# VectorE's order inside one step of a graph attention network: input statistics and mask sum at the head, score minima ahead of the norm, second statistics behind low half 6

## The reference, cut to what matters

```python
h = jnp.maximum(_layernorm(x, axis=-1), 0.0)
x = x + _L0_gnn_ref(h, adj, W_fc, W_attn)      # one attention layer
h = jnp.maximum(_layernorm(x, axis=-1), 0.0)
x = x + _L1_gnn_ref(h, adj, ...)               # three attention layers

# _L0_gnn_ref
h = graph_input @ W_fc.T;  f1 = h @ a1;  f2 = h @ a2
scores = leaky_relu(f1[:, :, None] + f2[:, None, :], 0.2)
attn = softmax(where(adj == 0, -1e9, scores), axis=2)
return elu(attn @ graph_input)

# _L1_gnn_ref, for each of the three layers l
si = x @ attn_w[l, :d];  sj = x @ attn_w[l, d:]
scores = leaky(si[:, :, None] + sj[:, None, :] + attn_b[l], 0.2)
attn = softmax(where(adj + eye > 0, scores, -inf), axis=-1)
h = layernorm(x + attn @ x, g1[l], beta1[l])
ff = gelu(h @ W1[l] + b1[l]) @ W2[l] + b2[l]   # 256 -> 1024 -> 256
x = layernorm(h + ff, g2[l], beta2[l])
```

## Time and profile before

| | |
|---|---|
| median of 3 runs | 2773.87 us (2773.44 to 2774.45) |
| the profiled execution | 2771.33 us, its span 2769.5 us |
| TensorE busy (matmul) | 2651.5 us, 96% of the span |
| ScalarE busy | 2200.2 us, 79% |
| VectorE busy | 2138.1 us, 77% |
| GpSimd busy | 1689.8 us, 61% |
| TensorE's mean granted clock | 0.985 of full speed |

### The profile page before, as it was taken

The page is one execution under the profiler, slowest core; times in us unless marked ns, Lnnn a source line. Parts: engine busy times, 40 slices in busy tenths (PEclk is TensorE's granted clock), DMA queues, the critical chain, the costliest instruction groups (busy, mean ns, idle before and its releaser), DMA issues.

```text
span 2769.5 us, 53308 instructions
## 1 busy us (share of the span) xinstructions
PE 2651.5 (96%) x16771; PEld 2386.7 (86%) x16868; DVE 2138.1 (77%) x7995; ACT 2200.2 (79%) x4494; POOL 1689.8 (61%) x2197
## 2 busy tenths in 40 slices
PE   3699999999999999999999999999999999999997
PEld 2488888988888989888888888889888998998997
DVE  5898878777878777878777878777878777676674
ACT  4699888888888888888887888888878777777774
POOL 4467666566766565566676666555677554454655
PEclk8699999999999999999999999999999999999999
DMA  5221322222222221122222122222222211111111
GB/s 177 90 70 62 95 81 92 66 79 76 87 81 77 66 71 62 64 70 88 85 90 69 65 67 76 69 68 68 80 89 91 62 45 52 35 52 52 51 64 54
DMA packets 118589, 203.43 MB, mean 73 GB/s; under 512 B 12800, under 2 KB 85536, under 8 KB 118304
## 3 DMA queue, kind: packets, MB, share of 16 engines
q1 hardware_dynamic: 118304, 199.97, 22.3%
HBM read 116.05 MB, written 83.89 MB: 72 GB/s over the span
## 4 chain that ended last, share of the span: by engine, by line
PE 71%; DVE 12%; POOL 8%; issue 5%; ACT 3%; DMA 0%; DVEq 0%; SPq 0%; POOLq 0%; ACTq 0%
PE bank L605 32%; PE bank L588 26%; PE ps_u L564 7%; POOL xo L374 3%; DVE g_lo L983 3%; DVE st L957 2%; PE ps_u L646 2%; POOL rs L1283 2%; DVE ub L1074 2%; PE ps_s L559 2%; PE ps_s L551 1%; POOL hb L374 1%; DVE vb L952 1%; DVE ub L952 1%; ACT g_hi L859 1%
## 5 line engine op out<-in xcount | busy, mean ns | idle before, releaser
L605 PE MATMUL bank<-w_hi,g_hi 128*128 128x256 f32 x3072 | 890.5, 290 | 15.3 <-DVE g_lo L983 15.1
L605 PE MATMUL bank<-w_hi,g_lo 128*128 128x256 f32 x3072 | 865.2, 282 | 0.0
L605 PE MATMUL bank<-w_lo,g_hi 128*128 128x256 f32 x3072 | 863.9, 281 | 0.0
L859 ACT ACTIVATE g_hi<-bank,b_eff 128x512 fp32r<-128x512 f32 x768 | 529.3, 689 | 334.4 <-PE bank L588 327.9
L983 DVE TENSOR_TENSOR g_lo<-bank,g_hi 128x512 fp32r<-128x512 f32 x768 | 518.9, 686 | 202.3 <-ACT bank L861 188.2
L588 PE MATMUL bank<-zt_hi,w_hi 128*128 128x512 f32 x1536 | 632.4, 412 | 12.0 <-DVE g_lo L983 5.6
L588 PE MATMUL bank<-zt_hi,w_lo 128*128 128x512 f32 x1536 | 607.7, 396 | 0.0
L588 PE MATMUL bank<-zt_lo,w_hi 128*128 128x512 f32 x1536 | 606.4, 395 | 0.0
L605 PEld LDWEIGHTS bank<-w_hi,g_hi 128*128 128x128 f32 x3072 | 578.9, 188 | 24.2 <-DVE g_lo L983 23.1
L605 PEld LDWEIGHTS bank<-w_lo,g_hi 128*128 128x128 f32 x3072 | 579.2, 189 | 0.8
L605 PEld LDWEIGHTS bank<-w_hi,g_lo 128*128 128x128 f32 x3072 | 578.7, 188 | 0.0
(11 more groups left out here) (95 smaller groups left out, 4145.8 us busy)
## 6 DMA issues: line engine op xcount, KB each, us to landing
xb<-x_scratch SPq DMA_DIRECT2D x88, 512.0 KB, 4.0
x_scratch<-xo SPq DMA_DIRECT2D x64, 512.0 KB, 4.8
xin<-in_x SPq DMA_DIRECT2D x38, 512.0 KB, 5.9
r_scratch<-elu_r SPq DMA_DIRECT2D x32, 512.0 KB, 3.0
xin<-r_scratch SPq DMA_DIRECT2D x32, 512.0 KB, 4.6
out<-xo SPq DMA_DIRECT2D x32, 512.0 KB, 3.4
m<-m_scratch SPq DMA_DIRECT2D x96, 128.0 KB, 3.8
x_scratch<-h SPq DMA_DIRECT2D x24, 512.0 KB, 2.9
```

What stands on the lines that cost most here:

```text
L605: mm = pe.matmul(y, g[:, c, r * P:(r + 1) * P], w[:, l, c, :], start=(c == 0 and n == 0), stop=(c == C - 1 and n == 2))
L859: act.activation(g_hi[:, c, :], block_in, ACT.Gelu, bias=bias).then_inc(g_hi_ready, 1)
```

## The change

VectorE's list is changed in all steps that don't take the first branch, so from step 5 on. `input_statistics()` (early steps) and `mask_sums()` (middle steps) move to the head of the step, ahead of `g_low(0)`. `input_variance()` moves up behind `first_variance()`, `input_shift()` behind `first_norm()`. `g_low(2)` now stands ahead of the score minima `next_lows()`, `g_low(3)` ahead of `first_norm()`. `second_statistics()` stands behind `g_low(6)`, which comes one place further forward, and `second_variance()` behind `g_low(7)`. GpSimd's list has the root of the input norm ahead of `scaled_rows()`. The lists of TensorE, ScalarE and SyncE are the same as before.

```diff
+                input_statistics()
+                if v1 is not None and early_step(v1) >= 0:
+                    mask_sums(v1)
                 g_low(0)
                 sum_rows()
                 g_low(1)
                 first_variance()
+                input_variance()
+                g_low(2)
                 next_lows()
-                g_low(2)
+                g_low(3)
                 first_norm()
-                g_low(3)
-                input_statistics()
+                input_shift()
                 g_low(4)
                 g_low(5)
+                g_low(6)
                 second_statistics()
-                g_low(6)
+                g_low(7)
                 second_variance()
-                g_low(7)
-                input_variance()
-                if v1 is not None and early_step(v1) >= 0:
-                    mask_sums(v1)
                 low_rows()
-                input_shift()
...
                 first_root()
                 if v3 is not None and v3 < CH:
                     made_root()
-                scaled_rows()
-                if v3 is not None and v3 < CH:
+                    scaled_rows()
                     input_root()
                     second_root()
                 else:
+                    input_root()
+                    scaled_rows()
                     second_root()
-                    input_root()
```

## The result

The changed kernel takes 2864.38 us (median of four runs, 2860.79 to 2870.03) against 2773.65 us (four runs, 2771.57 to 2774.45). The ratio is 1.033 (95% interval 1.0312 to 1.0348). The profiled execution took 2860.79 us with a span of 2859.0, that is 89.5 us more than the span before.

A forecast was written before the change was run, and what follows sets the result against it. TensorE, busy for 96% of the span, was taken to bound the kernel. 2771.33 (profiled execution) + 50 (early steps) + 19 (middle steps) = 2840, expected as a median of 2843; range for 8 in 10: 2813 to 2878.

The forecast's parts named there:

- the stall: Early steps: statistics wait for x, g_low(1) is late, TensorE stalls 2.7 us at hidden(4); +50 us over 23 steps.
- the middle steps: Middle steps: VectorE's lateness carries over and the mask sum loses its cover; 26.90 becomes 28.0, together +19 us.
- 2830 to 2862: The forecast case's own range for the whole kernel's time, chance 0.68.
- the clock rival: Early-step stalls each bring a stretch at half clock costing 1.65 us, 38 in all; time 2881, chance 0.12.
- three signs: Wrong if x statistics start within 1 us of vb, middle steps stay at 26.9, or the clock dips in early steps.
- The landing of x: Early steps: x lands 4.8 us into step 35, with 0.2 added on the mean for later loads.
- The landing that the Trainium skill: Early steps: x lands 3.2 us after its issue, stall 1.2 us shorter, sum some 27 us smaller.
- The rest at nothing: Late steps, steps without side work, GpSimd's moved root and SyncE's later xb load cost nothing.
- The rival on the other side: g_low(0) of early steps: x is there in time, leaving a gain of 27 us; 2746 in all, chance 0.04.
- The mask sum: Head of middle steps: the time behind g_low(7) that hid it is gone; 0.70 us plus 0.61 to the next start.

The follow-up runs named there:

- filler kernel: The changed kernel with eleven matmuls of 128x512 more ahead of hidden(4) in early steps, into a bank nobody reads then: 2843.28 us, ratio 1.0254.
- kernel without the wait: The changed kernel with the head statistics of early steps taken over old h0 rows already there, in place of x: 2764.15 us, ratio 0.9965.
- statistics put back: The changed kernel with statistics, variance and shift of x and GpSimd's input root back in their old places: 2783.34 us, ratio 1.0035.
- low halves kept: As statistics put back, with the mask sum and second statistics also behind g_low(7), so only the moved low halves 2 and 3 stay: 2779.92 us, ratio 1.0019.
- low halves alone: The kernel before with only g_low(2) moved ahead of the score minima and g_low(3) ahead of the norm: 2775.18 us, ratio 1.0004.

## Why the prediction was right, and where it was off

The forecast was 2843 with a range of 2813 to 2878, and slower with 0.94. Measured were 2864. Its cause is shown: with the moved statistics alone 86 us come, and with the wait alone taken away they go. Its sizes were off by 21 us, in three terms: +6 for the stall, +32 for the clock, -19 for the middle steps. The last 2 us lie outside the 69 steps.

That the total is no further off is in part luck, since two of these errors have opposite signs. The measured time lies above the forecast's own 2830 to 2862, and inside the wide range because that was drawn up towards the clock rival. Of the three signs that I had named for being wrong, two came: middle steps stay at 26.9, and the granted clock dips in the early steps. The late x was forecast rightly, what TensorE does behind its stall was not.

**The landing of x and the stall: right.** Forecast were 4.8 us into step 35, and 0.2 later on the mean. In step 35 VectorE's wait ended at 4.55. On the mean of all 23 it ended at 5.25 (the sum `vb` ends 0.91 into a step, and the row of waits gives 99.8 / 23 = 4.34 of waiting). At full clock a step is as long as this landing plus a constant: step 68 waited until 2102.96, 4.75 into the step, and took 29.06, so the constant is 24.31 (the other six steps at full clock give 24.30 to 24.31). With it 23 steps at full clock make 23 x (5.25 + 24.31) = 680 us. The filler kernel, which kept the clock, has 679.7. Against 624.3 before that is **+56**, where the sum had +50. The late landings, which the earlier trace rows told of, put the mean 0.7 behind step 35 and not 0.2; that step 35 itself came 0.25 sooner took a part of it back. The page after has nearly the same median:

```profile
xin<-in_x SPq DMA_DIRECT2D x38, 512.0 KB, 6.0
```

The landing that the Trainium skill (DMA: Bandwidth & Descriptors, Anatomy of one DMA) gave, by an estimate from its figures (1.2 us sooner, and 27 us off the sum), was not seen: no early step waited for less than 4.5 us into it.

**The clock: the step that failed.** The forecast said "granted clock still 1.00 from 135 us on" and gave 0.12 to the rival in which it falls. It fell in 16 of 23 early steps and costs 712.1 - 680 = **+32 us** there. Added up step by step it is 30; the rest is time that step 47, the last of the hardware loop's first turn, loses in the filler kernel too. The rival's own term was 38, from 1.65 a step in all 23. Ten falls cost about that, six cost 2.3 to 2.7 (step 32 is one, 32.70 long), and seven steps had none. The bound was the weak point: 2.45 us without work in step 47 had been harmless, and I took 2.8 for near it. But 2.45 is the sum of what step 47 had. The longest single wait of TensorE in the 69 steps of the kernel before is shorter (the view of the earlier trace rows):

```profile
PE bank L588 <- issue: 1.9, 1, 1.9
```

The waits for low half 1, 2.3 to 4.1 us each by the rows, were all longer, and not harmless in most cases. The kernel before had shown nothing about a single wait of this length. The Trainium skill (TensorE: Matmul & The Clock Gate, Why this matters for your kernels) says that idle gaps bring the engine back to the lower clock; 16 steps agree with it, seven with waits as long do not.

**The middle steps: mis-sized, +19 forecast and 0 measured.** The delay of the chain was right. GpSimd's `hb` (answers to the earlier trace rows) was forecast for 1117.6, 15.5 into step 35, and starts 15.0 into it:

```profile
1159.01 2.84 POOL L374 TENSOR_TENSOR hb<-ub,g_row 128x256 f32<-128x256 f32 x4 [2.02 <-DVE ub L1074]
```

`nm` of the second norm stood 19.12 into step 35 before, and stands 22.29 into it now, 3.17 later (3.2 forecast), with 9.88 to `vb` behind it (9.99 forecast):

```profile
1166.30 0.16 DVE L973 SCALAR_TENSOR_TENSOR nm<-mv,rs 128x4 f32<-128x4 f32 x1
...
1176.18 1.29 DVE L1180 TENSOR_TENSOR vb<-bank,hb 128x512 f32<-128x512 f32 x2
```

But TensorE was late as well, and by more: step 35 grew by 3.4 us, so `vb` starts 1.77 into step 36 and not at the forecast 3.25, and that step takes the 26.90 of before. Where the clock held, the lateness did arrive, at less than half the size forecast: step 15 takes 27.35 and not 28.0.

```profile
541.25:570.66 29.41, 26.48 (x171) 23.69 (x170) 22.77 (x88) 21.86 (x44) 17.33 (x22) 1.00 0.28 86
570.66:598.01 27.35, 27.10 (x176) 24.23 (x175) 23.84 (x96) 23.56 (x51) 18.57 (x24) 1.00 0.21 73
```

There the step before had grown by 2.6, nearly as much as VectorE was late. With the clock kept everywhere (the filler) the middle steps cost +11. The layer-2 middle steps gained 2.6 us together (step 18 takes 27.51), which pays for steps 6, 9 and 12, of 0.4 us more each, for step 15, and for step 48, of 1.1 more. So two of my terms were tied: what the clock adds in an early step it takes from the middle step. Together they are +32 and -11. The forecast's 2843 is what the filler kernel measured (2843.28): where the clock holds, stall and middle steps make 66 us (1974.17 - 1907.94), against the 69 of the sum.

**The rest at nothing: right.** Late steps take 28.44, the steps from 74 on 26.3.

**The rival on the other side: its price was wrong.** If x had been there in time I gave 2746, a gain of 27 us made of all the waits for low halves. The kernel without the wait has 2764, the one with only the low halves moved 2780. The early and the middle step are bound as a pair by VectorE's and GpSimd's chain from the norm to `vb`. What TensorE no longer waits for in the early step, it waits for at `vb` in the middle step, unless that chain is made shorter too. This error of mine showed in four expectations: statistics put back (2754 expected, 2783 measured), low halves kept (2756 and 2780), low halves alone (2766 and 2775), and the kernel without the wait.

**The mask sum: the reason was right.** Its cover was gone at the head of a step. By itself it costs 7 us, half of it in the layer-2 middle steps, and in the changed kernel the middle steps lose 7.7 by it.

**Still open.** Why one wait brings the lower clock and another, as long, does not, was not settled. It does not lie in the step alone: step 65 kept its clock in the changed kernel and lost it in the traces of the statistics alone and of the mask sum put back. That in step 35 the clock fell because of the wait and not of something beside it rests on the filler, where the same wait of VectorE left the clock at 1.00.

## What to carry to other kernels

Before an instruction is moved ahead, look up when its operand lands, and not only whether the engine has idle time there: on an engine with a fixed order, a wait is worth what is queued behind it. A removed wait is a gain only where nothing else binds over the same span, so add up the chain of the slower engine over two neighbouring steps before you price it. And where TensorE is given a new pause of a few us, expect the clock to take its share on top, though not each time. Here `hidden(4)` came 2.5 to 4.3 us later in 23 steps, 74 us in all, and the clock cost some 30 more. Compare such a pause with the longest single pause that was harmless, not with a step's idle time added up.

## What was not expected of the hardware

- The granted clock fell behind a wait of TensorE of 2.3 us (step 35) and held through a longer one (step 65, which takes 30.17 us at 1.00). In step 35 it fell 0.5 us behind the end of the wait, while TensorE was already at work again; in step 32 it fell 1.8 us before the end.
- Eleven matmuls of 128x512 that nobody needs (2.72 us in step 35) made the kernel 21 us faster.
- The same load of 512 KB, from the same place of the program and issued 0.4 us into the step both times, had landed 4.5 us into step 35 and 6.1 into step 32. The median over the run hides this spread.
